# The message layers of a graph network: attributes placed in PSUM by ScalarE, messages summed as a rounded part and its exact rest

## The reference, cut to what matters

```python
x = x + attention_layer(relu(layernorm(x)))
h = relu(layernorm(x))
for i in range(3):
    msg  = relu(h[src] + edge_attr)                 # 200000 x 128
    aggr = segment_sum(msg, dst, num_segments=6250)
    t = relu(bn((h + aggr) @ W1[i] + b1[i]))
    h = bn(t @ W2[i] + b2[i])                       # relu too, but in the last layer
return x + h
```

## Time and profile before

| | |
|---|---|
| time, median of 3 runs | 4708.72 us (4705.17 to 4715.48) |
| profiled execution | span 4705.4 us, 143705 instructions |
| PE busy | 4259.9 us, 91% of the span |
| PE weight loads | 4143.3 us, 88% |
| DVE busy | 4028.4 us, 86% |
| ACT busy | 2654.7 us, 56% |
| POOL busy | 3384.3 us, 72% |
| `sum_half` products (L1798) | 1520.3 us |
| `gather` products (L1784) | 1142.0 us |

### The profile page before, as it was taken

One profiled execution on the slowest core, in us unless ns is written; L12 is line 12 of the kernel. 1 busy time (PEld: TensorE's weight loads), 2 busy tenths in 40 slices (PEclk: granted clock), 3 DMA queues, 4 the chain that ended last, 5 costly groups with the idle time before them and its releaser, 6 DMA issues.

```text
span 4705.4 us, 143705 instructions
## 1 busy us (share of the span) xinstructions
PE 4259.9 (91%) x50439; PEld 4143.3 (88%) x50440; DVE 4028.4 (86%) x7870; ACT 2654.7 (56%) x6749; POOL 3384.3 (72%) x2584
## 2 busy tenths in 40 slices
PE   3566776899999999789999998999999979999998
PEld 2566666899999999789999996999999969999997
DVE  7899997677777777689999997899999879999997
ACT  3899997577777777644444445344444454444444
POOL 0488886777777777367878772778778638778773
PEclk7777777899999999889999998999999989999999
DMA  9988844788888888578888884888888748888884
GB/s 140 271 299 268 289 164 142 221 250 253 249 242 252 252 250 242 154 249 289 288 286 289 285 285 146 275 289 287 283 289 286 269 156 288 287 290 286 286 285 151
DMA packets 664741, 1183.55 MB, mean 252 GB/s; under 512 B 151850, under 2 KB 489596, under 8 KB 664588
## 3 DMA queue, kind: packets, MB, share of 16 engines
q1 hardware_dynamic: 450204, 839.07, 54.4%
q10 hardware_dynamic: 133200, 176.14, 15.3%
q0 software_dynamic: 81184, 166.43, 10.7%
HBM read 967.32 MB, written 214.44 MB: 251 GB/s over the span
## 4 chain that ended last, share of the span: by engine, by line
PE 76%; DVE 12%; issue 5%; SPq 4%; DMA 2%; ACT 1%; POOL 0%; DVEq 0%; ACTq 0%; POOLq 0%; PEld 0%; PEldq 0%
PE ps L1798 26%; PE ps L1784 18%; PE ps L1713 13%; PE ps L1700 11%; PE ps L1808 7%; DVE sums L1179 2%; DVE field L1179 2%; PE ps L1850 1%; DVE blk_hot L1171 1%; DVE scan L1216 1%; DVE rank L1233 1%; DMA unit_x<-gin_rows,unit_src 1%; DVE pos_hot L1190 1%; DVE unit_x L1459 1%; DVE bn L1592 0%
## 5 line engine op out<-in xcount | busy, mean ns | idle before, releaser
L786 POOL DMA_INDIRECT unit_x<-gin_rows,unit_src x1449 | 1915.0, 1322 | 483.4 <-issue 382.4
L741 POOL DMA_INDIRECT attr_by_slot<-abuf,ridx x1080 | 1406.1, 1302 | 464.5 <-issue 328.6
L1798 PE MATMUL ps<-dst_hot,sums 128*128 128x128 f32 x10584 | 1520.3, 284 | 13.4 <-ACT sums L981 11.8
L981 ACT ACTIVATE sums<-sums 128x512 f32<-128x512 f32 x1512 | 833.3, 572 | 1193.2 <-DVE sums L1483 1188.0
L1798 PEld LDWEIGHTS ps<-dst_hot,sums 128*128 128x128 f32 x10584 | 1306.4, 192 | 31.9 <-DVE agg L1492 16.7
L1784 PE MATMUL ps<-x_parts,src_turned 128*128 128x128 bf16 x15876 | 1142.0, 220 | 29.4 <-POOL x_parts L773 21.3
L1784 PEld LDWEIGHTS ps<-x_parts,src_turned 128*128 128x128 bf16 x15876 | 1025.8, 99 | 48.8 <-issue 29.5
L1483 DVE TENSOR_TENSOR sums<-ps,sums 128x512 f32<-128x512 f32 x1512 | 904.2, 616 | 179.9 <-PE ps L1784 179.5
L893 ACT ACTIVATE val<-ps,val 128x128 f32<-128x128 f32 x2597 | 717.9, 375 | 187.0 <-DVE val L1325 186.6
L1475 DVE TENSOR_TENSOR dst_hot<-iota_one,dl_slot 128x896 f32<-128x896 f32 x756 | 817.6, 1082 | 2.1 <-DVE agg L1528 2.1
L1713 PE MATMUL ps<-val,src_hot 128*128 128x129 f32 x5194 | 694.7, 283 | 2.2 <-DVE sums L1263 1.0
(11 more groups left out here) (243 smaller groups left out, 4369.8 us busy)
## 6 DMA issues: line engine op xcount, KB each, us to landing
sums<-attr_by_slot SPq DMA_DIRECT2D x756, 448.0 KB
src_turned<-rows_by_group SPq DMA_DIRECT2D x756, 224.0 KB, 5.3
turned_hot<-rows_by_block ACTq DMA_DIRECT2D x392, 384.0 KB
attr_by_slot<-zeros SPq DMA_DIRECT2D x36, 3136.0 KB
unit_attr<-in_edge_attr SPq DMA_DIRECT2D x204, 448.0 KB
abuf<-in_edge_attr SPq DMA_DIRECT2D x72, 960.0 KB
unit_x<-gin_rows,unit_src POOLq DMA_INDIRECT x1449
attr_by_slot<-abuf,ridx POOLq DMA_INDIRECT x1080
```

The source lines that it names most:

```text
L741: pool.indirect_dma_start(out=attr_table, out_offset=bass.IndirectOffsetOnAxis(ap=ridx[:, g, t0 + t:t0 + t + 1], axis=0), in_=abuf[:, k % ...
L786: pool.indirect_dma_start(out=unit_x[:, half_place(k), t, :], out_offset=None, in_=gin_rows[n], in_offset=bass.IndirectOffsetOnAxis(ap=uni ...
L981: act.activation(attr[:, first:first + tiles, :], attr[:, first:first + tiles, :], ACT.Relu).then_inc(s_msg, 1)
L1798: ins = pe.matmul(ps[:, 7, 0:WINDOW], attr[:, b, :], dst_hot[:, HOT[c], b % G_TILES, :], start=(b == 0), stop=(b == BLOCKS - 1))
```

## The change

- ACT copies a half's attributes into its PSUM bank (`seed`, four halves ahead), and the gather adds onto them: all gather matmuls run with `start=False`. Once in a layer PE opens the six banks with six matmuls of zeros, 512 columns wide.
- ACT's `message` reads PSUM, takes the relu and writes it rounded to `float32r`. DVE's `split_message` writes relu of the same PSUM less the rounded part, also `float32r`. A bank is free for the next seed when this has been done.
- `sum_half` now holds the one-hot stationary and streams the two parts as 256 columns: one `float32r` matmul to a block. The window comes out in bank 7 the other way round, so ACT copies it to SBUF (`keep_window`, after `message(2)` of the next group), PE turns and sums the two parts into bank 6 (`turn_window`), and DVE adds it to `agg` at half 5. The first sum of a group waits for `keep_window` of the one before.
- The parts lie in three places of a chunk each, `split_msg`, where `nodes` was; `nodes` is stored to HBM before the layers and loaded back after the last group.
- Unit sums move from halves 4 and 11 to 6 and 11. The attributes' reload waits for the seed instead of the sum.

```diff
@@ scalar engine
+                def seed(i, h):
+                    first, tiles = half_of(h)
+                    if h % 2 == 0:
+                        act.wait_ge(s_attr[h // 2], 16 * (n * BUCKETS + i + 1 + cleared(h // 2)))
+                    before = bank_user(h)
+                    if not (isinstance(i, int) and i == 0 and before < 0):
+                        act.wait_ge(s_low, lows_done(n, i, before))
+                    act.activation(ps[:, BANK[h], 0:tiles * D].rearrange("p (b d) -> p b d", d=D), attr[:, first:first + tiles, :], ACT.Copy).then_inc(s_seed, 1)
 
                 def message(i, h):
-                    act.wait_ge(s_pre, G_HALVES * n * BUCKETS + G_HALVES * i + h + 1 + BANKS)
-                    act.activation(attr[:, first:first + tiles, :], attr[:, first:first + tiles, :], ACT.Relu).then_inc(s_msg, 1)
+                    act.wait_ge(s_gath, halves_before + G_HALVES * i + h + 1 + G_HALVES)
+                    act.wait_ge(s_used, halves_before + G_HALVES * i + 2 * place_user(c) + h % 2 + 1 + G_HALVES)
+                    to = split_msg[:, SPLIT_PLACE[c], 0, inner, :]
+                    act.activation(to, ps[:, BANK[h], 0:tiles * D].rearrange("p (b d) -> p b d", d=D), ACT.Relu).then_inc(s_msg, 1)
+
+                def keep_window(g):
+                    act.wait_ge(s_used, halves_before + G_HALVES * (g + 1) + G_HALVES)
+                    act.activation(window_out[:, :, :].rearrange("p k d -> p (k d)"), ps[0:WINDOW, 7, 0:2 * D], ACT.Copy).then_inc(s_wout, 1)
...
                         message(i, h)
+                        if h == WINDOW_OUT_AT and not (isinstance(i, int) and i == 0):
+                            keep_window(i - 1)
+                        if h + SEED_LEAD < G_HALVES:
+                            seed(i, h + SEED_LEAD)
+                        elif more:
+                            seed(i + 1, h + SEED_LEAD - G_HALVES)
                         c = h // 2 + PART_LEAD
                         if parts and h % 2 == 1 and c < G_CHUNKS:
                             second_part(n, c)
...
@@ vector engine
-                def add_attributes(i, h):
-                    vec.wait_ge(s_gath, halves_before + G_HALVES * i + h + 1 + G_HALVES)
-                    vec.tensor_tensor(attr[:, first:first + tiles, :], ps[:, BANK[h], 0:tiles * D].rearrange("p (b d) -> p b d", d=D),
-                                      attr[:, first:first + tiles, :], ALU.add).then_inc(s_pre, 1)
+                def split_message(i, h):
+                    vec.wait_ge(s_msg, halves_before + G_HALVES * i + h + 1)
+                    vec.scalar_tensor_tensor(split_msg[:, SPLIT_PLACE[c], 1, inner, :], ps[:, BANK[h], 0:tiles * D].rearrange("p (b d) -> p b d", d=D), 0.0,
+                                             split_msg[:, SPLIT_PLACE[c], 0, inner, :], ALU.max, ALU.subtract).then_inc(s_low, 1)
@@ tensor engine
-                        ins = pe.matmul(ps[:, 7, 0:WINDOW], attr[:, b, :], dst_hot[:, HOT[c], b % G_TILES, :],
-                                        start=(b == 0), stop=(b == BLOCKS - 1))
+                        ins = pe.matmul(ps[:, 7, 0:2 * D].rearrange("p (k d) -> p k d", d=D), dst_hot[:, HOT[c], b % G_TILES, :],
+                                        split_msg[:, SPLIT_PLACE[c], :, b % G_TILES, :], start=(b == 0), stop=(b == BLOCKS - 1))
+                def turn_window(g):
+                    for k in range(2):
+                        ins = pe.matmul(ps[:, 6, 0:WINDOW], window_out[:, k, :], ident[:, :], start=(k == 0), stop=(k == 1))
@@ sync engine
+            sp.wait_ge(s_var, 2)
+            sp.dma_start(node_rows, nodes[:, :, :].rearrange("p b d -> p (b d)")).then_inc(s_node_rows, 16)
```

More of the change, by code:

```diff
@@ L88, with place_user @@
 ADD_AT = 3
-SUM_AT = 4
-KEEP_AT = 2
-WINDOW_AT = 2
+SUM_AT = (6, 11)
+KEEP_AT = (9, 0)
+WINDOW_OUT_AT = 2
+WINDOW_TURN_AT = 3
+WINDOW_AT = 5
 LOAD_AT = 6
+SPLIT_PLACE = (0, 1, 2, 0, 1, 2, 1)
+SPLIT_PLACES = max(SPLIT_PLACE) + 1
+def place_user(c):
+    return c - next(d for d in range(1, 8) if SPLIT_PLACE[(c - d) % 7] == SPLIT_PLACE[c])
 U = 7
@@ L1005, in group_of @@
                             message_of_unit(i, unit_at(i, h))
-                group_of(0, True)
-                group_of(1)
+                act.wait_ge(s_bank, n + 1)
+                for h in range(SEED_LEAD):
+                    seed(0, h)
+                group_of(0, True, parts=True)
+                group_of(1, True)
                 with act.Fori(2, BUCKETS - 1) as i:
-                    group_of(i)
-                group_of(BUCKETS - 1)
+                    group_of(i, True)
+                group_of(BUCKETS - 1, False)
+                keep_window(BUCKETS - 1)
                 def keep(m, c):
@@ L1539, in group_of @@
                             point_targets(i, c)
-                        add_attributes(i, h)
+                        split_message(i, h)
                         if h == 0:
@@ L1784, in gather @@
                             ins = pe.matmul(ps[:, BANK[h], k * D:(k + 1) * D], src_turned[:, b * P:(b + 1) * P], x_parts[:, part, b, :],
-                                            start=(k == 0 and part == 0), stop=(k == tiles - 1 and part == PARTS - 1))
+                                            start=False, stop=(k == tiles - 1 and part == PARTS - 1), skip_group_check=True)
                     ins.then_inc(s_gath, 1)
@@ L1824, in group_of @@
                         sum_half(i, h)
-                        if h % BY_UNIT == SUM_AT and unit_at(i, h) is not None:
+                        if h == WINDOW_TURN_AT and not (isinstance(i, int) and i == 0):
+                            turn_window(i - 1)
+                        if h in SUM_AT and unit_at(i, h) is not None:
                             if isinstance(i, int) and i == LEFT_GROUP:
@@ L1828, in group_of @@
                             sum_unit(i, unit_at(i, h))
+                nothing = zeros[:, :].bitcast(BF16)
+                for bank in range(BANKS):
+                    ins = pe.matmul(ps[:, bank, :], nothing[:, 0:P], nothing[:, 0:CHUNK], start=True, stop=True)
+                ins.then_inc(s_bank, 1)
                 for h in range(G_LEAD):
```

74 lines of the change are left out of this document (52 added, 22 removed).

## The result

| | before | after |
|---|---|---|
| time, median of 5 runs each | 4709.07 us (4705.17 to 4715.48) | 4737.42 us (4728.10 to 4751.23) |
| ratio | | 1.0066, 95% interval 1.0048 to 1.0084 |
| profiled execution, span | 4705.4 us | 4747.5 us (its time 4749.24) |

The change costs 28 us; 91 were forecast. The two profiled spans are 42 us apart, because that execution of the changed kernel lies at the slow end of its five.

What follows compares the result with a forecast made beforehand. PE was taken as the bound, with DVE only 9% behind. Terms of 62 (unit groups), +22 (group 0), -6 (stretches without units), +7, +2 and +2 made +89 us: 4800 us, chance 0.53, range 4600 to 4920.

Steps and rivals of the forecast that it cites:

- rival B: PE's clock drops in the gaps between splits, PE late by about 1 us a group: +103, 4900 us; chance 0.13.
- the group with units: Groups with unit sums: 23.75 us against 23.1, 0.6 longer, over 103 groups +62 us (bounds +10 and +145).
- DVE's own work, "21.1": DVE's work in a group without its waits for PE, 23.1 - 2.0 = 21.1 us, taken as unchanged.
- the waits for ACT, "2.65": DVE's new waits per group: 1.5 us at half 11, 0.65 at half 4, then 0.35 and 0.15 behind them.
- Group 0: "+22": First group of a layer: each chunk loses 1.1 plus 0.35 us, 5 chunks in 3 layers, +22 us.
- "+7": Layer start: opening the banks and a first seed, 3.2 us in layers 2 and 3, 1 in the first.
- Ends of a layer, `nodes`: "+4": Window copy and turning at layer ends, +2 us; storing `nodes` to HBM, mostly hidden, +2 us.
- PE: "17.6 us" a group: PE's work in a group falls from 23.1 to 17.6 us, with sum matmuls at 0.12 us; it leaves the bound.
- Rival A (relief gets through): DVE's waits at the units stay under 1.7 us a group, so faster: 4633 or 4530 us; chance 0.25.
- E (no change): Gains and losses meet, no change that can be told: 4708 us; chance 0.05.
- C: PE's message sum costs more than one pass: 5100 us at two passes, 5950 at the f32 price; chance 0.03.
- D: DVE's `split_message` runs at half throughput, +6.5 us a group: 5500 us; chance 0.01.

Runs made afterwards that it cites:

- Experiment 1: Changed kernel with ACT's unit relu moved behind messages 5 and 11: 4582.16 us; or cut to one of seven blocks: 4588.40 us (kernel before, same cut: 4718.08 us).

## Why the prediction was right or wrong, point by point

- **Direction and mechanism: right.** PE left the bound; the relief did not get through, because DVE's waits for PE were replaced by round trips through ACT at the units. Experiment 1 shows it by removing them. But about half of what was lost in the groups with units came another way, by the clock (rival B, below), which the forecast had put at nothing.
- **The failed step: the group with units, 23.75 us forecast, 23.23 measured.** It carried 62 of the 89 us and came to 20.4, and only 11.9 of these by the longer ordinary group. The mechanism was right and two sizes were off, together by 0.5 us on a difference of 0.6; the 11.0 us from the clock, not in the forecast's sum, brought it nearer by luck. First, DVE's own work, "21.1", is 20.8: I had subtracted from the group before only the three waits that the timeline labels. Most of the difference is a start without a label, the unit's window (L1510) at 3212.43, late by 0.23 us behind a `turn_sources` that began at 3211.84 and took 0.44; the rest, under 0.1 us, I could not place with certainty. Second, the waits for ACT, "2.65", are 2.44: 1.48 at half 11 (1.5 forecast), 0.58 at half 4 (0.65), 0.28 at half 5 (0.35), 0.10 at half 13 (0.15). These were read from the durations in the trace and each is right within 0.1.
- **Group 0: "+22", of which the chunks gave about 11.** The waits came as forecast but for 0.1 to 0.2 us (0.98 and 0.21 of idle, 1.35 with lost overlap, against 1.45). What I kept at its old price was `rest`: 1.71 us before, 1.08 after, since it no longer runs beside POOL's subtraction (before, POOL's L773 ran from 2919.91 to 2921.97 and `rest` started at 2921.21; now POOL's L806 runs from 2932.52 and `rest` has ended at 2931.46). A chunk is 0.72 us longer, not 1.45. The start of the layer took the rest:

```profile
2918.62 2.74 PE L1913 MATMUL ps<-zeros 128*128 128x512 bf16 x6 [1.26 <-DVE flat L1677]
...
2924.21 0.69 DVE L1547 SCALAR_TENSOR_TENSOR split_msg<-ps,split_msg 128x512 fp32r<-128x512 f32 x1 [3.56 <-ACT split_msg L1030]
```

  The opening cost 2.74 us (2.6 forecast) and DVE stood 3.52, 3.56 and 3.24 us before its first split of the three layers, 10 us where "+7" stood. Groups 0 and 1 together came to +19.4, near what was forecast for them, by errors that cancel.
- **Ends of a layer, `nodes`: "+4", measured about +2**, no more than the reading allows.
- **PE: "17.6 us" a group, measured 19.2.** A sum instruction is 0.143 us and not 0.12, between the bounds given; that makes 18.7, and the other 0.5 I did not place. In the ordinary group it cost nothing, as PE has room; and it may have kept the clock up. The prediction says that no row shows the passes of an f32 matmul; the earlier trace rows do, with 0.24 us a block against 0.056 for a bf16 one of the same width, 4.3 times.
- **Rival A (relief gets through)** is what one moved line would have given: DVE 569 of 600 us busy and 4582 us. **B (clock)** happened in part: 26 of the 99 groups fell to 0.93 or 0.94 and lost 0.4 us each, 11 us where B had put 1 us a group and 103 us. The mean of 0.98 mid-layer hides it, and the sign of being wrong that the prediction named (under 0.95) would have passed over it. With two parts to the gather it comes in full (0.88). **E (no change)** is out by its interval, though it was nearer in size than the forecast. **C** is out (0.143 us an instruction, where two passes were put at 0.24), **D** too:

```profile
L1547 DVE SCALAR_TENSOR_TENSOR split_msg<-ps,split_msg 128x512 fp32r<-128x512 f32 x179 | 122.0, 682 | 12.5 <-ACT split_msg L1030 12.5
L1030 ACT ACTIVATE split_msg<-ps 128x512 fp32r<-128x512 f32 x178 | 104.5, 587 | 19.9 <-PE ps L1851 19.9
```

  The split takes the 682 ns of the add that it replaced. The halved throughput with two non-bf16 SBUF sources is the one rule of the Trainium skill that spoke against the change (Vector Engine (DVE) Microarchitecture Reference, Points that are easy to get wrong), and the measurement decides against applying it here, where one source is PSUM and the other f32 in SBUF.

## What to carry to other kernels

When two engines are near the bound, relief on one is worth only what the handshakes of the other allow: look for an engine that waits for an answer from a queue in which something long stands ahead of the answer, and move that thing behind it before anything is removed. A forecast that is the difference of two near sums (waits gone, waits come) needs the small waits counted too, those of 0.1 to 0.3 us with no label. A mean clock hides single groups: read it group by group. And work taken off TensorE is no safe gain: look at the granted clock of each stretch, and at the engine that is full next.

## What the runs showed of the hardware that was not expected

- Two kernels from which a third of the gather matmuls was taken became 1.2 to 1.7% slower; in the changed kernel's case each long group shows a granted clock of 0.79 to 0.93.
- In the changed kernel TensorE's clock fell to its lower level 26 times 1.6 to 2.3 us after a stand of 1.26 to 1.28 us, and 72 times it did not after the same stand.
- GpSimd's indirect gathers pause every 112 gathers, which are eight groups here, for 3.3 to 6.0 us, in three kernels at the same gather; a larger lead did not move it, and straight code with more instructions has shorter stops (2.1 to 4.0 us) in most of the same places.
- A `float32r` matmul costs 0.143 us at 256 columns and 0.117 at 128; an f32 one of 128 columns costs 0.24, in two instructions.
- VectorE's subtraction of 128x896 f32 took 1.71 us beside a GpSimd subtraction and 1.08 without.
